# Cross-attention of a small transformer block on one core: the first half of the next V directly behind the next K, the transposes of the probabilities behind that half

## The reference

```python
x = x + _L0_xattn_ref(_layernorm(x), ctx_1024, mask, Wq, bq, Wkv, bkv, Wo, bo)
# in it, with H = 16 heads of 32:
q = x @ Wq + bq                              # (32, 32, 512)
k, v = jnp.split(context @ Wkv + bkv, 2, -1) # (32, 257, 512) each
q = _larope(q, Lq); k = _larope(k, Lk)       # rotation by position
scores = jnp.einsum('bhqd,bhkd->bhqk', q, k) * SCALE
attn = jax.nn.softmax(where(mask, scores, -inf), axis=-1)
out = jnp.einsum('bhqk,bhkd->bhqd', attn, v) @ Wo + bo
```

## Time and profile before

| | us |
|---|---|
| median of 3 runs | 805.36 |
| lowest, highest | 801.39, 805.53 |
| the profiled execution | 800.47 |
| its span, first to last instruction | 798.5 |
| TensorE busy in the span | 765.1 (96%) |
| DVE, ScalarE, GpSimd busy | 488.3, 340.4, 215.9 |
| TensorE's mean granted clock | 0.983 of full |

### The profile page before, as it was taken

The page is one execution under the profiler, slowest core; times in us unless marked ns, Lnnn a source line. Parts: engine busy times, 40 slices in busy tenths (PEclk is TensorE's granted clock), DMA queues, the critical chain, the costliest instruction groups (busy, mean ns, idle before and its releaser), DMA issues. The chain is left out here.

```text
span 798.5 us, 21613 instructions
## 1 busy us (share of the span) xinstructions
PE 765.1 (96%) x9096; PEld 641.8 (80%) x9097; DVE 488.3 (61%) x1109; ACT 340.4 (43%) x812; POOL 215.9 (27%) x192
## 2 busy tenths in 40 slices
PE   8999999999999999999999999999899998699992
PEld 7888888889888898888988889887677776587770
DVE  6656575566655657456566465757889987622227
ACT  6433534335334354343533445435377653133330
POOL 0222223212232222321232222321232230245540
PEclk9999999999999999999999999999999999899995
DMA  8622001000010001100011000202942337634438
GB/s 310 258 81 81 29 29 54 28 29 29 31 52 28 29 29 36 47 28 29 29 52 31 28 29 28 107 9 83 386 160 95 128 122 275 242 120 158 154 119 319
DMA packets 22397, 78.07 MB, mean 98 GB/s; under 512 B 3224, under 2 KB 3736, under 8 KB 19360
## 3 DMA queue, kind: packets, MB, share of 16 engines
q1 hardware_dynamic: 18624, 64.66, 22.2%
q0 software_dynamic: 3680, 12.06, 4.5%
HBM read 58.10 MB, written 18.61 MB: 96 GB/s over the span
## 5 line engine op out<-in xcount | busy, mean ns | idle before, releaser
L154 PE MATMUL bank<-chi,wparts 128*128 128x258 f32 x496 | 143.7, 290 | 0.0
L156 PE MATMUL bank<-chi,wparts 128*128 128x258 f32 x496 | 140.1, 282 | 0.0
L155 PE MATMUL bank<-clo,wparts 128*128 128x258 f32 x496 | 140.0, 282 | 0.0
L327 POOL TENSOR_TENSOR pdiag_hi<-p_last_and_rinv_hi,const 128x256 fp32r<-128x256 f32 x32 | 19.8, 617 | 328.6 <-DVE p_last_and_rinv_hi L574 328.6
L321 POOL TENSOR_TENSOR ksin<-kb,const 128x1032 f32<-128x1032 f32 x32 | 95.0, 2968 | 41.2 <-ACT kb L374 41.2
L779 PE MATMUL bank<-wparts,chi 128*128 128x512 f32 x256 | 105.8, 413 | 0.0
L154 PEld LDWEIGHTS bank<-chi,wparts 128*128 128x128 f32 x496 | 93.5, 188 | 12.8 <-issue 12.8
L780 PE MATMUL bank<-wparts,chi 128*128 128x512 f32 x256 | 101.3, 396 | 0.0
L781 PE MATMUL bank<-wparts,clo 128*128 128x512 f32 x256 | 101.1, 395 | 0.0
L366 ACT ACTIVATE chi<-craw 128x1032 fp32r<-128x1032 f32 x32 | 34.2, 1070 | 146.4 <-PE bank L781 144.2
L550 DVE TENSOR_TENSOR v<-bank,bias_cross 128x512 f32<-128x512 f32 x64 | 43.9, 689 | 83.9 <-PE bank L781 83.9
(11 more groups left out here) (269 smaller groups left out, 1632.1 us busy)
## 6 DMA issues: line engine op xcount, KB each, us to landing
craw<-ctx_t_dram SPq DMA_DIRECT2D x32, 516.0 KB, 3.4
expert_lo<-weights_dram SPq DMA_DIRECT2D x8, 1024.0 KB, 13.2
expert_hi_scratch<-wraw SPq DMA_DIRECT2D x16, 512.0 KB, 3.0
wparts<-expert_hi_scratch SPq DMA_DIRECT2D x8, 1024.0 KB, 8.8
wraw<-weights_dram SPq DMA_DIRECT2D x7, 1024.0 KB, 5.8
expert_lo<-ffn_out_scratch SPq DMA_DIRECT2D x16, 256.0 KB, 4.9
x<-x_dram SPq DMA_DIRECT2D x8, 256.0 KB, 7.7
ffn_xn_scratch<-xn SPq DMA_DIRECT2D x8, 256.0 KB, 2.1
```

The lines of the kernel that those rows point to most:

```text
L154: pe.matmul(psum, ahi(c), bhi(c), start=(c == 0), stop=False)
L155: pe.matmul(psum, ahi(c), blo(c), start=False, stop=False)
L156: last = pe.matmul(psum, alo(c), bhi(c), start=False, stop=(c == chunks - 1))
```

## The change

In the step's loop on TensorE the call of `probs_transposed(b)` moves two calls down: behind the first half of V (or, in the very last step, behind the second product of the self-attention).

```diff
@@ -897,11 +897,11 @@
                                 k_product(b + 1, j + 1, m)
                         else:
                             self_product(0)
-                        probs_transposed(b)
                         if more:
                             v_product(b + 1, j + 1, 0)
                         else:
                             self_product(1)
+                        probs_transposed(b)
                         if j == 0 and first:
                             v_last_product()
                         if j == 0 and not first:
```

## The result

| | before | after |
|---|---|---|
| median, us | 804.17 (4 runs) | 833.33 (4 runs) |
| lowest to highest | 801.39 to 805.53 | 831.60 to 836.58 |
| ratio, with its 95% interval | | 1.0369 (1.0331 to 1.0408) |
| profiled execution, us (span) | 800.47 (798.5) | 833.34 (831.5) |

The forecast was 831, between 822 and 840.

A forecast was written before the change was run, and what follows sets the result against it. TensorE, busy 399.95 of 400 us, was taken to bound the kernel, so new pauses add one for one: 30 x 0.89 + 0.56 = 27.3 us on 800.5 or 805.4 gives 827.8 or 832.7; named 831, range 822 to 840.

The forecast's parts named there:

- views 1 and 2: Busy time by stretch (TensorE 399.95 of 400 us) and TensorE's list of waits (one loop entry, 0.8 us once).
- (a): V's first half directly behind K: doesn't wait, stays 2.86 us; 0.08 taken as price of going from transpose to 512-column matmul.
- (b): Transposes of the probabilities 2.8 us later: more room behind the exp is worth nothing, their issues still cost 0.79 us.
- (c): Item behind the transposes waits for ScalarE's four evacuations, starting at 1.68 instead of 0.79: 0.89 us lost in 30 steps.
- (d): Restart behind the wait: +0.03 us in 15 steps, saving up to 0.08 in 15; together nothing, within 1 us.
- (e): Steps t=7: j=2 costs 0, covered by V's second half; at j=3 the attention product starts 0.56 us late.
- (f): Next scores and K products: V's second half lies between as before, banks come free in time, so nothing is late.
- The sum: Over the cross-attention loop: 30 x 0.89 + 0.56 = 27.3 us, bounds 22.6 and 38.4, none of it hidden.
- Serial evacuations: Rival: ScalarE's four evacuations don't overlap, each step loses up to 1.25 us: 38.4, so 839 to 844; chance 0.08.
- The clock in every step: Rival: TensorE's clock falls in each of 30 steps, 1.4 us per dip, 42 us more, about 873; chance 0.05.
- A shorter pause: Rival: the bank's semaphore comes without the chain, each step loses about 0.4 us: 12 us, 813 to 817; chance 0.04.
- Not slower, the delay being taken up at the boundary: Rival: next stage's loads run beside the longer cross-attention at its end; time stays 801 to 805; chance 0.03.

The follow-up runs named there:

- experiments 1 and 3: Against the kernel before: transposes inside V's first half, two chunks behind them (805.86 us) or one (812.02); and changed order, waiting item moved behind V's second half (810.13 us).

## Why the prediction was right

**What bounds (views 1 and 2): right.** TensorE had no pause in the loop, each new pause went to the end.

**(a) V directly behind K: right.** No wait; the second matmul of V follows the first by 0.22 us (176.00 to 176.22), where it was 0.31 behind a transpose.

**(b) Transposes later: right.** Their place alone costs and gains nothing (experiments 1 and 3).

**(c) The new wait: right in its place and mechanism, a little small.** By its own steps: ScalarE's start at 0.42, as worked out. The end of the fourth evacuation at 1.63 for 1.62: the pitch between the first and second was 0.28 instead of 0.26 and the three took 0.93 for 0.94. The hand-over from ScalarE to TensorE was the term that was mis-sized: 0.10 us at the output product, where the row I took it from had 0.06. At the transposes of x it was 0.14 (order of time, step b=9):

```profile
197.31 0.38 PE L803 MATMUL bank<-const,pr 128*128 128x128 f32 x2
...
199.08 0.63 PE L711 MATMUL quad<-const,xn 128*128 128x128 f32 x4 [0.74 <-ACT pt L389]
```

```profile
198.01 0.93 ACT L389 ACTIVATE pt<-quad 128x256 f32<-128x256 f32 x3
```

From 198.94 to 199.08. So the item starts at 1.73 to 1.77 for 1.68, and the loss is 0.94 to 0.98 before the savings of (d), for 0.89. Over the 30 steps the loop grew by 0.94 each.

**(d) Starting again: right.** The steps grew by 0.90 to 0.97 where the item moved by 0.94 to 0.98; the remainder is within 0.1 us per step, some 1 us in all.

**(e) The last two steps: right in the waits, a little large in the price.** At t=7, j=2 there is no wait. At j=3 the attention product starts 1.69 us behind the first transpose (574.52 to 576.21) for 1.68, so it is 0.57 us late for 0.56. TensorE, order of time:

```profile
574.52 0.38 PE L803 MATMUL bank<-const,pr 128*128 128x128 f32 x2
...
576.21 0.76 PE L815 MATMUL quad<-pt,v 128*32 128x32 f32 x64 [0.41 <-ACT pt L389]
```

The 0.41 is only the visible part of it, from the modelled end of the diagonals. The stage's end moved by 0.47 for this step and not by 0.56: the products' first matmul, 0.32 us from its successor behind the transposes, now follows another product and saves the 0.08 of (a), which (e) left out.

**(f) Nothing is late next: right.** No new releaser appears in the list.

**The sum:** 28.7 us in the loop for 27.3, and 29.7 by the ratio. TensorE's visible waits are 31 with 22.2 us, for "about 30" and "some 20".

**The rivals.** Serial evacuations: no, they overlap (0.93 for three of 0.39). The clock in every step: no, 1.00 from 50 to 500 us with a pause in every step, and in the first step it fell as before (0.91 over 30 to 50 us in both traces). By the Trainium skill, "TensorE: Matmul & The Clock Gate", section "A second HAM failure mode: psum-queue depth-cycling", a price on top was to be feared; pauses of 0.7 us, once in 16 to 19 us, did not bring it about here. A shorter pause: no. Not slower, the delay being taken up at the boundary: no, the boundary moved back by 29.5 us. SyncE waits there 16.8 us where it waited 16.3.

One assumption did not hold: the 831 was put between two levels of 800.5 and 805.4 us that I read out of four executions. The further runs of before fill the room from 799.7 to 807.3, so there are no two levels, only a spread, which the experiments found in the first step's clock (1.6 us) and, again with the clock, behind the boundary (5 us). That 831 lies so near is in part luck: the sum on the median of before as it came out, 804.2 + 27.3 = 831.5, happens to meet a value that was picked between the two supposed levels.

## What to carry to other kernels

Where the busiest engine has no waits, a change of order on it can't gain from waits; it can only lose cover, so look for what the moved piece was covering. Here the transposes' place had to be at least one evacuation chain (1.75 us from the first transpose) ahead of the first instruction that writes one of their banks, and anything between counts off that number one for one. If such a chain must stand open, let the bank that is written next be evacuated first and wait for it alone: that took the loss from 29.7 to 7.0 us with the transposes left where they were.

## What the runs showed of the hardware that I had not expected

- The fall of TensorE's clock behind the narrow matmuls at 37 to 40 us differs between executions of one program: 0.91 over 30 to 50 us in one, 1.00 in the next, 1.6 us apart.
- Behind the boundary the same 1992 matmuls were granted a clock of 0.93 to 0.95 from one execution to another, and the stretch took 249.8 to 244.5 us.
- From ScalarE's end to TensorE's start there are 0.06, 0.10 and 0.14 us in three places. What sets this was not tried.
- A copy of 256 columns out of a bank starts 0.27 us behind another though its row is 0.39 long; two inserted between others, each with a wait for the one before, added 0.69 us and not twice their length.
